# One fused block on one core: a rewritten preparation, attention products issued between two heads, and maximum items spread differently over the steps

## What is computed

```python
xn = layernorm(x)                                  # x: 4 sequences x 1024 rows x 128
q, k, v = (xn @ Wq.T, xn @ Wk.T, xn @ Wv.T)        # 16 heads of 8 columns
q, k = rope(q, k)                                  # q*cos + rotate_half(q)*sin
scores = where(causal, -inf, q @ k.T / sqrt(8))
att = softmax(scores) @ v  @ Wo.T
p = softmax(xn @ router_w.T)                       # 8 experts, the best 2 are kept
moe = sum over the 2 experts of weight * (relu(xn @ w1.T + b1) @ w2.T + b2)
out = x + att + moe
```

## Time and profile before

| | us |
|---|---|
| median of 3 runs (lowest, highest) | 820.54 (819.13, 821.37) |
| the profiled execution, its own time | 819.88 |
| its span, first to last instruction | 817.9 |
| first exponential of unit 0 | 151.60 after the start |
| units 3 to 7 and 9 to 11, each | 29.2 |
| unit 12 with the experts | 176.8 |

### The profile page before, as it was taken

The page is one execution under the profiler, slowest core; times in us unless marked ns, Lnnn a source line. Parts: engine busy times, 40 slices in busy tenths (PEclk is TensorE's granted clock), DMA queues, the critical chain, the costliest instruction groups (busy, mean ns, idle before and its releaser), DMA issues.

```text
span 817.9 us, 19208 instructions
## 1 busy us (share of the span) xinstructions
PE 704.2 (86%) x5654; PEld 418.5 (51%) x5654; DVE 577.7 (71%) x977; ACT 448.5 (55%) x1089; POOL 258.5 (32%) x305
## 2 busy tenths in 40 slices
PE   2887337689799999999789999899999999989897
PEld 1455323334344445444334435499999983534344
DVE  5454289688577788788577788666666667999434
ACT  3722010266466676666556676667666655657541
POOL 3344240266557512111102112100000006767731
PEclk9988555599989999999989999999999998999689
DMA  8045968315653263134032133022222225111724
GB/s 232 32 135 136 194 145 245 59 48 92 242 93 70 63 169 58 17 63 57 14 58 39 26 61 52 16 61 68 70 67 67 68 70 78 45 46 47 176 74 138
DMA packets 60743, 71.40 MB, mean 87 GB/s; under 512 B 9790, under 2 KB 47902, under 8 KB 60474
## 3 DMA queue, kind: packets, MB, share of 16 engines
q1 hardware_dynamic: 56588, 62.18, 33.5%
q0 software_dynamic: 4096, 8.40, 3.8%
HBM read 41.11 MB, written 26.67 MB: 83 GB/s over the span
## 4 chain that ended last, share of the span: by engine, by line
PE 56%; DVE 6%; ACT 6%; DMA 2%; issue 2%; POOL 1%; SPq 0%; ACTq 0%; DVEq 0%; POOLq 0%
PE bank L1142 16%; PE bank L1157 15%; PE bank L1199 8%; PE bank L1217 8%; ACT probs L702 6%; PE bank L1118 5%; DVE mx L864 4%; PE bank L1125 2%; DMA k_high<-slots_out_d,slot 1%; DMA stack<-mrow 1%; PE bank L1208 1%; PE bank L1240 1%; PE bank L1254 1%; POOL k_high L591 1%; DVE xn_all L932 1%
## 5 line engine op out<-in xcount | busy, mean ns | idle before, releaser
L702 ACT ACTIVATE probs<-bank 128x512 f32<-128x512 f32 (+3 forms) x768 | 318.6, 493 | 238.6 <-PE bank L1142 235.8
L864 DVE TENSOR_REDUCE mx<-bank 128x2 f32<-128x1024 f32 (+3 forms) x320 | 344.4, 1114 | 81.1 <-PE bank L1125 68.8
L1142 PE MATMUL bank<-stack 64*128 64x512 f32 (+3 forms) x768 | 240.7, 443 | 40.5 <-ACT probs L702 21.3
L1142 PEld LDWEIGHTS bank<-stack 64*128 64x128 f32 x768 | 109.7, 193 | 221.7 <-ACT probs L702 159.0
L608 POOL TENSOR_SCALAR_AFFINE_SELECT probs<-probs 128x512 f32<-128x512 f32 x128 | 81.6, 639 | 440.6 <-ACT probs L702 440.2
L1118 PE MATMUL bank<-stack 64*128 64x512 f32 (+3 forms) x768 | 178.9, 405 | 6.1 <-DVE mx L864 5.9
L1157 PE MATMUL bank<-probs,vst 128*32 128x512 f32 (+3 forms) x1536 | 171.2, 519 | 1.8 <-POOL probs L608 1.6
L1118 PEld LDWEIGHTS bank<-stack 64*128 64x128 f32 x768 | 89.1, 201 | 14.0 <-DVE mx L864 13.2
L1199 PE MATMUL bank<-tiles_s,staged 128*128 128x128 f32 x576 | 77.9, 278 | 0.8 <-ACT tiles_s L707 0.8
L1125 PE MATMUL bank<-masks_b 64*128 64x128 bf16 (+1 forms) x1024 | 77.9, 219 | 0.0
L1217 PE MATMUL bank<-staged,q_high 128*128 128x128 f32 x576 | 76.2, 275 | 0.5 <-DVE k_high L965 0.5
(11 more groups left out here) (116 smaller groups left out, 434.6 us busy)
## 6 DMA issues: line engine op xcount, KB each, us to landing
stack<-parts_d SPq DMA_DIRECT2D x96, 128.0 KB
slots_in_d<-probs SPq DMA_DIRECT2D x1, 4608.0 KB, 20.5
tiles_s<-slots_in_d SPq DMA_DIRECT2D x72, 64.0 KB, 1.8
slots_out_d<-k_high SPq DMA_DIRECT2D x72, 64.0 KB, 1.5
early<-in_w_experts SPq DMA_DIRECT2D x1, 4112.0 KB
parts_d<-early SPq DMA_DIRECT2D x8, 512.0 KB, 5.1
stack<-parts_d SPq DMA_DIRECT2D x64, 64.0 KB
heads_d<-xnT SPq DMA_DIRECT2D x124, 18.0 KB
```

The source lines that it names most:

```text
L702: nc.scalar.activation(probs[n % 3][:, h, q0:HALF], st_of(at)[:, 0:HALF - q0], ACT.Exp, scale=SCALE).then_inc(s["probs_made"], 1)
L864: v.tensor_reduce(to, src.rearrange("p g (a k) -> p g a k", k=w), AX_X, ALU.max, negate=True).then_inc(s["scores_read"], 1)
L1142: mm(st_of(at)[:, 0:HALF - q0], kstk[r][g][:, hp, kb * P:(kb + 1) * P], qstk[r][g][:, hp, c * HALF + q0:(c + 1) * HALF], start=True, stop=True
```

## The change

There are three parts.

1. *The preparation* is unrolled over the four sequences and has two sets of buffers (the second in the `probs` tiles and in `tiles_s`, `[b % 2]`). DVE writes the normalised rows straight into `xn_all`, so SP's copy goes. PE uses two PSUM pairs instead of four: pair 0 for the transposed rows, the logits, qs and ks, pair 1 for q, k and v, each product waiting for the reader before it. The logits come first, and the transposes of the next sequence directly behind the values. The statistics and `normalise` of the later sequences are spread over the first two. A sine or a rounding waits for the parts of two sequences earlier. SP stores each part as it is ready, loads a stack after sequences 0 to 2 instead of 1 to 3, and writes the slots' zeros in four quarters, one per sequence, from a tile in `const_s`. ACT clears one stack per sequence; its first exponential waits for all parts to be stored rather than for the zeros; POOL's first scattering waits for the zeros. The first 9 of the 20 items of unit 0 are made and read inside sequences 2 and 3 (`PREPARED`), behind a wait for stack 0. `keep_warm` issues products of a tile of ones (128x512, bf16) into a bank that nobody reads: 28 at the start, 30 ahead of the counting of tokens, one after each of the 11 items that are left, 6 before the turning of the maxima and 16 before the first score.
2. *The products* of a step are issued between the scores of heads 2 and 3 rather than at the end of the step. In step 7 the maxima are turned behind head 3, and items follow.
3. *The items*: step 7 now has two, of the unit after next (`FIRST` 8 to 7), and `TILES_OF_STEP` has one item fewer in steps 2 and 10.

```diff
--- before.py
+++ after.py
@@ -142,19 +142,18 @@
...
+        xnTs = [xnT[:], tiles_s[:].rearrange("p t c -> p (t c)")]
...
+        zeros = const_s[:, P:2 * P]
+
+        turned_q, turned_k, rope_q, rope_k = (
+            [early[:, NT * C + i * S:NT * C + (i + 1) * S], spare[i // 2][:, i % 2 * S:(i % 2 + 1) * S]]
+            for i in range(4))
+        high_q, high_k = [q_high[:], spare[2][:, 0:S]], [k_high[:, 0:S], spare[2][:, S:2 * S]]
...
-        FIRST, TURN = 8, 7
+        FIRST, TURN = 7, 7
         LEAD = 2
-        TILES_OF_STEP = [2, 2, 2, 1, 2, 2, 2, 0, 2, 2, 2, 1]
+        TILES_OF_STEP = [2, 2, 1, 1, 2, 2, 2, 2, 2, 2, 1, 1]
...
+        PREPARED = {(2, "k"): 1, (2, "ks"): 1, (2, "v"): 1, (3, "logits"): 1, (3, "q"): 1, (3, "qs"): 1, (3, "k"): 1,
+                    (3, "ks"): 1, (3, "v"): 1}
...
+        WARM = [28, 30, 1, 6, 16]
...
-            def keep_rows(b):
-
-                sp.wait_ge(s["xn_ready"], b + 1)
-                sp.dma_start(xn_all[:, b * T:(b + 1) * T, :], xn).then_inc(s["xn_kept"], 16)
...
+                for first, n, part, tile in (("q_first", 0, 0, high_q[b % 2]), ("k_first", 1, 0, high_k[b % 2]),
+                                             ("q_split", 0, 1, rope_q[b % 2]), ("k_split", 1, 1, rope_k[b % 2])):
+                    sp.wait_ge(s[first], b + 1)
+                    sp.dma_start(parts_d[n, b * G:(b + 1) * G, :, part, :, :].rearrange("g h d s -> (g h) d s"), tile
+                                 ).then_inc(parts_written[n][b % 2], 16)
...
+            def load_ones(i):
+
...
+                for g in range(2):
...
+            def zero_slots(i):
+
+                tiles = slice(i * TILES // 4, (i + 1) * TILES // 4)
+                sp.dma_start(slots_in_d.rearrange("(j p) c -> p j c", p=P)[:, tiles, :],
+                             zeros.unsqueeze(1).broadcast_to([P, TILES // 4, C])).then_inc(s["slots_zeroed"], 16)
...
-            keep_rows(0)
+            sp.wait_ge(s["rows_ready"], 1)
+            sp.dma_start(zero_rows_d.rearrange("n (t q) -> n t q", q=P), zero_rows).then_inc(s["zeros_stored"], 16)
             for b in range(B):
...
                 keep_parts(b)
...
+                    for written in parts_written:
+                        sp.wait_ge(written[0], 16 * PARTS)
+                if b == 0:
                     sp.wait_ge(s["zeros_stored"], 16)
-                    for written in parts_written:
...
+                if b < 3:
+                    load_ones(b)
+                    load_stacks(b, b)
+                if b == 0:
+                    sp.wait_ge(s["zeros_ready"], 1)
+                zero_slots(b)
+            load_ones(3)
             for written in parts_written:
...
+                    sp.wait_ge(written[i], 16 * PARTS * 2)
             store_max_rows(0, 0)
...
+            pool.memset(ones_b[:], 1.0).then_inc(s["ones_ready"], 1)
...
+                i = b % 2
...
+                for first, r, high, split_done in (("q_first", rope_q[i], high_q[i], "q_split"),
+                                                   ("k_first", rope_k[i], high_k[i], "k_split")):
+                    pool.wait_ge(s["roped"], 2 * b + 2)
...
+            pool.memset(mrow[1][:], 1.0).then_inc(s["rows_ready"], 1)
...
+            pool.sem_inc(s["consts_ready"], 1)
+            for b in range(B):
                 split(b)
...
+            pool.wait_ge(s["slots_zeroed"], 16 * 4)
...
+                if b >= 2:
+                    act.wait_ge(s["v_made"], b - 1)
+                nc.scalar.copy(xnTs[b % 2], pair[0]).then_inc(s["xnT_ready"], 1)
...
+                    act.wait_ge(parts_written[n][b % 2], 16 * PARTS)
+                act.wait_ge(s["roped"], 2 * b + n + 1)
+                nc.scalar.copy(tile[b % 2].bitcast(F32R), r[b % 2]).then_inc(s[first], 1)
...
+            roots(0)
+            roots(1)
+            turned(0)
+            keep_logits(0)
+            roots(2)
             act.wait_ge(s["zeros_ready"], 1)
             clear_stack(0)
...
+            for b in range(B):
+                high(b, 0)
+                keep_values(b)
+                if b + 1 < B:
+                    turned(b + 1)
+                if b == 0:
+                    roots(3)
+                    nc.scalar.activation(table_s[:, 1:2], eps_s[:], ACT.Exp).then_inc(s["table_loaded"], 1)
+                high(b, 1)
+                if b + 1 < B:
+                    keep_logits(b + 1)
+                    clear_stack(b + 1)
+            act.wait_ge(s["rt_shifted"], 1)
+            nc.scalar.activation(rt[1], rt[0], ACT.Exp).then_inc(s["rt_exped"], 1)
...
+            for written in parts_written:
+                act.wait_ge(written[1], 16 * PARTS * 2)
...
+                dve.wait_ge(s["ln_std"], b + 1)
...
+                if b >= 2:
+                    dve.wait_ge(s["roped"], 2 * (b - 2) + n)
+                v.tensor_tensor(t[b % 2], ps, cos_s, ALU.mult).then_inc(s[used], 1)
...
+                if b >= 2:
+                    dve.wait_ge(written[b % 2], 16 * PARTS)
+                v.tensor_tensor(r[b % 2], ps, sin_s, ALU.mult).then_inc(s[used], 1)
...
             row_stats(0)
             normalise(0)
             row_stats(1)
+            normalise(1)
+            dve.wait_ge(s["tab_loaded"], 16 * 2)
+            cos_q(0)
             row_stats(2)
+            sin_q(0)
+            normalise(2)
+            cos_k(0)
             row_stats(3)
-            dve.wait_ge(s["tab_loaded"], 16 * 2)
-            sequence(0)
-            with dve.Fori(1, B - 1) as b:
-                sequence(b)
-            sequence(B - 1)
-
+            sin_k(0)
+            for b in range(1, B):
+                early_items(b, "logits")
+                cos_q(b)
+                early_items(b, "q")
+                sin_q(b)
+                early_items(b, "qs")
+                if b == 1:
+                    normalise(3)
+                cos_k(b)
+                early_items(b, "k")
+                sin_k(b)
+                early_items(b, "ks")
+                early_items(b, "v")
...
+                if isinstance(u, int) and u == 0:
+                    dve.wait_ge(s["zeros_stored"], 16)
+                if isinstance(u, int) and u == 1:
+                    for i in range(4):
+                        dve.wait_ge(stack_loaded[i], 32 + 12 * 16)
...
+                    if j == TURN and more(u, 1):
+                        copy_rows(u + 1, (r + 1) % 4)
...
+            for n in range(sum(PREPARED.values()), NI):
...
+            def keep_warm(n, to):
+
+                for _ in range(n):
+                    mm(bank[:, to, :], ones_b[:], ones_b[:].unsqueeze(1).broadcast_to([P, CK, P]), start=True, stop=True)
...
+                for n in items_at(b, stage):
+                    if n == 0:
+                        pe.wait_ge(stack_loaded[0], stack_count(0, 0))
+                        pe.wait_ge(s["consts_ready"], 1)
+                    score_item(0, 0, n)
...
                 for t in range(T):
...
+                early_items(b, "logits")
+                if b:
+                    pe.wait_ge(s["v_copied"], b)
+                project_rows(b, 0, 1, "q_made")
+                early_items(b, "q")
+                pe.wait_ge(s["logits_copied"], b + 1)
+                project_rows(b, 1, 0, "qs_made")
+                early_items(b, "qs")
                 pe.wait_ge(s["q_used"], b + 1)
+                project_rows(b, 2, 1, "k_made")
+                early_items(b, "k")
+                pe.wait_ge(s["qs_used"], b + 1)
+                project_rows(b, 3, 0, "ks_made")
+                early_items(b, "ks")
...
+                early_items(b, "v")
+                if b + 1 < B:
+                    turn_rows(b + 1)
...
+                        if h == HG - 1:
+                            products(u, r, j)
                         if more(u, ahead):
                             score(u + ahead, (r + ahead) % 4, n, h)
-                        if h % 2 and todo:
+                        if h % 2 and todo and j != TURN:
                             score_item(*todo.pop(0))
+                    if j == TURN and more(u, 1):
+                        turn_max(u + 1, (r + 1) % 4)
                     for item in todo:
                         score_item(*item)
-                    if j == TURN and more(u, 1):
-                        turn_max(u + 1, (r + 1) % 4)
-                    products(u, r, j)
...
+            pe.wait_ge(s["ones_ready"], 1)
+            keep_warm(WARM[0], 0)
...
+            for b in range(B):
+                sequence(b)
...
+            keep_warm(WARM[1], 3)
+            count_tokens()
+            for n in range(sum(PREPARED.values()), NI):
                 score_item(0, 0, n)
+                keep_warm(WARM[2], 3)
+            keep_warm(WARM[3], 3)
             turn_max(0, 0)
             pe.wait_ge(stack_loaded[1], stack_count(1, 1))
...
+            keep_warm(WARM[4], 3)
             pe.wait_ge(mrow_stored[0], mrow_count(0, 0))
             pe.wait_ge(s["routed"], 1)
```

256 lines of the change are left out of this document (93 added, 163 removed).

## The result

The changed kernel takes **809.47 us** (median of 4 runs, 807.52 to 811.57) beside 820.68 for the kernel before: a ratio of 0.9866, 95% interval 0.9834 to 0.9899. The prediction was 768.5 with a range from 752 to 792: the direction was right, the size was wrong by 41 us (11.2 us gained where 52 were forecast). The profiled execution took 810.79, its span is 809.1.

The account below looks back on a forecast made before the run. PE was taken to bound middle units, with 151.60 us of preparation in front where engines take turns. Gains of 28.5 (preparation), 3 (unit 0's clock) and 20.6 (units) sum to 52.1 us, giving 768.5, range 752 to 792.

Parts of the forecast that it names:

- the last normalising between its second and third factor, in front of the values: Preparation, sequence 1 on DVE: taken as 3.3 us (seen at 2.14 and 5.78), so that sequence 1 ends at 50.2.
- now sit among the first one's sines and cosines on DVE: Start of the preparation: later sequences' statistics and normalising share DVE with sequence 0; sequence 1's rows still turned at 31.4.
- The 2 us for the clock: Preparation: allowance for PE not being at the full clock throughout, 2 us, bounds 0 and 33.
- rival B: PE stays at the lower clock in the preparation: 780 at mean 0.75, 801 at half; chance 0.14, with rival A 0.05.
- the warming products add nothing: Preparation: warming products run while PE waits for the router, the reads or `routed`, so they cost 0 us.
- The tail: End of the preparation, from the last read of items to the first exponential: 10.9 us, as before.
- C: Rival: slower by the DMA queues, ACT's first exponential waiting for all parts; 835 us at 100 GB/s; chance 0.03.
- The term of 3 us: Unit 0: of 4.3 us lost to the lower clock level, 3 us regained, bounds 0 and 4.3.
- the ring of three banks: Wide step of a unit: score, exponential, return to PE, head 2 and products ask for 2.41 us, under PE's sum.
- PE's sum of 2.46: Wide step with products between heads 2 and 3: PE's work sets 2.46 us rather than 2.83.
- rival A: The units gain nothing, as products part heads 2 and 3 and cost what packing saves: 789 us; chance 0.16, with rival B 0.05.
- two narrow items enter step 7 and fill its wait: Middle units: steps 2 and 10 lose about 0.4 us each, steps 7 to 9 grow some 0.4 together; PE's work unchanged.

Follow-up runs that it names:

- norm_only: prep_dve with ACT's second square root ahead of the first copy of turned rows again, as in the changed kernel: 786.94 us, 0.9592 of before.
- prep_products2: Changed kernel with the old spread of items (none in step 7), products still between heads 2 and 3: 800.72 us, 0.978 of before.
- item_warm0: prep_dve without the one warming product behind each of the 11 items left: 780.48 us, 0.9499 of before.
- best2: prep_dve without warming products behind the 11 items and with 34 instead of 16 before the first score: 779.94 us, 0.9462 of before.
- after_again: The changed kernel unaltered, measured again beside a kernel before of 818.10 us: 806.84 us, 0.985 of before.
- prep_dve: prep_products2 with DVE's third and fourth normalising behind the last sines of sequences 0 and 1, ACT's first copy before the second square root: 783.04 us, 0.954.
- warm_more: prep_dve with 34 instead of 16 warming products before the first score: 781.10 us, 0.9516 of before.
- best: item_warm0 with the products at the end of the step in units 0, 1, 2, 12, 13 and 14: 781.76 us, 0.9535 of before.
- prep_only: Changed kernel with the old plan of items and products at the end of the step, the new preparation alone: 849.4 us, 0.9766 of before.

## Why the prediction was wrong

By the profiles, the front gained 18.5 us where 28.5 were forecast, unit 0 lost 0.5 where it was to gain 3, and units 1 to 15 lost 9.1 where they were to gain 20.6: together 43.3 of the 52.1 us. Each step that failed follows.

**The start and the sequences** (router forecast at 82, measured at 93.84). The failed step is "the last normalising between its second and third factor, in front of the values", for which I took 3.3 us, and that the later sequences' statistics and normalising "now sit among the first one's sines and cosines on DVE", for which I took nothing. Each of the two normalisings costs 4.2, and PE does not catch up: it waits 3.5 and 3.4 us and then runs at half the clock. Sequences 1 to 3 started at 38.8, 59.4 and 76.3 rather than at 33.7, 50.2 and 64.9. The 2 us for the clock were too few; it was 0.75 in the mean, the mild form of rival B, whose 11 us are near the 11.8 that the router started late. That rival gave as its reasons the waits for DVE and for ACT; the first is what the rows show, in sequences 0 and 1. The cause is the order on DVE: norm_only differs in it alone from prep_products2 (91.56 and 130.91), and its router starts at 80.67 and its first exponential at 119.66. Over all profiles the two groups don't touch: with the old order, seven kernels, the router starts at 91.6 to 96.4 and the first exponential comes at 130.9 to 135.8; with the new one, eight kernels, at 75.7 to 82.9 and 114.7 to 121.5, against my 82 and 123.1.

**Router, items, tail.** The router took 14.2 us to the first item rather than 18.0: DVE's wait for the exponential went to 0.48, and three operations that took 2.0, 2.4 and 2.0 us take 0.42 (two others, the subtraction of the maximum and a product, take 1.86 and 1.17 instead of 0.42). In both kernels all the slow ones ran beside an operation of POOL's: the three beside those that started at 103.55, 105.93 and 109.72, and at their place in the changed kernel POOL has no such operation left. I had not forecast this: 3.8 us of luck, which hides a part of the front's miss. The items took 14.2 rather than 12.2: the warming product behind each makes PE the bound at half the clock (item_warm0), and "the warming products add nothing" failed by 1.6 us. The tail was 10.9 as forecast. No transfer was late, no store was waited for by DVE, stack 0 was there in time: the moved transfers cost nothing, and C is out.

**Unit 0's clock.** The term of 3 us was near in size (36.00 before, 33.46 in best2 at the full clock) and wrong for this kernel: the 16 products end 4.12 us before the first score, the first eight products with the values take 1.93 us instead of 1.07, so PE is back at the lower level, and unit 0 grew by 0.50. Its mean clock was even a little higher than before (0.91 against 0.88), so the clock is not all that sets its length; what else does stays open.

**Products between heads 2 and 3.** PE's wait for ACT behind head 2 went, as forecast, and one term of the ring of three banks was mis-sized. I had 1.17 for head 3 to head 2, and measured 1.18; 1.00 for the products, and measured 1.00; but for head 2 alone 0.24, and it holds PE for 0.42 (340.17 to 340.59). The ring then asks for 2.60, more than PE's sum of 2.46, and 2.60 it is, to 0.01 us. A score takes 0.23 only with a neighbour in the other half of the rows; the products behind head 2 need all of them. The Trainium skill, TensorE: Matmul & The Clock Gate, "Part 3: Packing small matmuls — row/col tiling", lets neighbours in different row groups overlap; the trace agrees, and the parted head pays 0.18 for it. So a part of rival A was in force. With the old items a middle unit took 28.5: 0.7 less, half of what I forecast. The three wide steps of unit 6 gave 0.43 of it (intervals 2.80, 2.61 and 2.60 instead of 2.84, 2.83 and 2.77), not 1.1, and the nine others 0.23 together, some shorter and one longer (2.63 instead of 2.41); the "0.1 to 0.3" for each narrower step did not come.

**The items.** The step "two narrow items enter step 7 and fill its wait" failed. The wait of the kernel before lies ahead of head 3, and the items behind the turning, which is behind head 3. PE over that step in the kernel before:

```profile
364.29 0.44 PE L1142 MATMUL bank<-stack 64*128 64x384 f32 x1 [0.41 <-ACT probs L702]
364.66 0.33 PE L1132 MATMUL bank<-const_s,mneg 128*128 128x128 f32 x1
364.92 1.06 PE L1157 MATMUL bank<-probs,vst 128*32 128x512 f32 x8
```

PE's instructions start here in the order in which they are issued: the items came behind the turning, the turning behind the head that waited. They could not fill that wait, and the products filled it already. Each item there costs 0.5 us in full and ACT starves meanwhile. I had also counted them as neutral in units 13 and 14; there they cost 4.7 us (after_again beside prep_products2). So middle units lost 0.2 where I had a gain of 1.5, and units 12 to 14 lost 10.8. Of these, 4.8 are unit 12, whose 176 to 182 us followed the clock (0.95 to 1.00) in every kernel of the three later chips, and which took 176.26 in the changed kernel's second profile: that part is chance, and why the clock varies there stays open.

## What to carry to other kernels

Before a wait is said to be filled, find the instruction that waits and check that the filler is issued ahead of it; else it is added in full. Work moved into the sequence of an engine that another waits on costs its own time, and here the other's clock as well: put it behind the last operation that is waited for. And an instruction that is cheap because of its neighbour has to be priced alone when the neighbour is taken away.

## What was not expected of the hardware

The clock repeats badly. prep_dve and warm_more have the same instructions up to the warming products before the first score, and the same windows of 64 us gave PE 58.05 and 54.06 us of busy time:

```profile
20.00:84.00 64.00, 58.05 (x288) 33.54 (x287) 49.82 (x77) 31.89 (x27) 35.98 (x16) 0.89 0.72 181
```
```profile
20.00:84.00 64.00, 54.06 (x296) 31.79 (x296) 52.42 (x71) 31.76 (x27) 39.97 (x18) 0.97 0.76 187
```

At a clock of 0.89 and 0.97 the router started at 81.33 and 75.68. It is not only the chip: item_warm0 and best, on the chip of warm_more and with the same front up to the router, had it at 80.24 and 80.43. A single profile of this kernel's front is good to some 6 us.

DVE's eight normalising operations took 2.14 us with POOL idle, 4.2 beside one operation of POOL's and 8.45 beside three, which kept their 2.35 to 2.42 each:

```profile
27.97 8.45 DVE L791 TENSOR_SCALAR xn_all<-early,staged 128x128 f32<-128x128 f32 x8
```

By the Trainium skill, SBUF — State Buffer, "Who interferes with whom", a tensor_scalar in a two-port mode and a GpSimd instruction exclude each other. The times fit it, 2.14 and nearly POOL's whole time; in which mode these ran no row shows.

On the first chip of the experiments all kernels, that of before included, were some 50 us slower, in the units with scatters and gathers alone. ACT's timeline in unit 0 of prep_only:

```profile
152.53 0.59 ACT L720 ACTIVATE probs<-bank 128x512 f32<-128x512 f32 x1
159.22 2.08 ACT L720 ACTIVATE probs<-bank 128x512 f32<-128x512 f32 x4 [6.10 <-remote]
```

It waits 6.10 us for a count of PE's products, the last of which had started by 150.81; DVE's copy, which waits for the same count, started at 159.13 too. POOL issued the last of 11 scatters at 156.19. All four kernels of this chip have such waits, which the trace puts down to "remote", 47 to 84 us over ACT and DVE, and none of the 13 profiles of the other chips has one. Their cause stays open.
